# Rotary tables scaled per tile, a residual moved ahead of the maxima, and layer-norm statistics and root each moved one turn later

## The reference

```python
def ref(x, ...):
    xn = _layernorm(x)
    return x + attn(xn) + ffn(xn)        # attn: 16 heads of 8, causal, once

def ffn(x, ...):
    for i in range(6):                   # DEPTH
        x = attn_layer(shift_tokens(x), Wqkv[i], q_scale[i], k_scale[i], Wo[i]) + x
        x = ffn_layer(shift_tokens(x), ln_g[i], ln_b[i], W1[i], b1[i], W2[i], b2[i]) + x
    return x

def attn_layer(x, Wqkv, qs, ksc, Wo):    # 16 heads of 64, windows of 32
    q, k, v = split(x @ Wqkv)
    q, k = l2norm(q) * qs, l2norm(k) * ksc
    q = q * cos * scale + rotate_half(q) * sin * scale
    k = k * cos / scale + rotate_half(k) * sin / scale
    return local_attention(q, k, v) @ Wo # softmax over own and previous window

def ffn_layer(x, g, bln, W1, b1, W2, b2):
    xn = (x - mean(x)) / sqrt(var(x) + 1e-5) * g + bln
    a, gate = split(xn @ W1 + b1)
    return a * gelu(gate) @ W2 + b2
```

## Time and profile before

| what | value |
|---|---|
| median of 3 runs | 2076.58 us (2074.1 to 2080.54) |
| the profiled execution | 2091.56 us |
| its span | 2089.8 us |
| TensorE matmul busy | 91% of the span |
| VectorE busy | 80% |
| GpSimd busy | 70% |
| ScalarE busy | 63% |

### The profile page before, as it was taken

The page is one execution under the profiler, slowest core; times in us unless marked ns, Lnnn a source line. Parts: engine busy times, 40 slices in busy tenths (PEclk is TensorE's granted clock), DMA queues, the critical chain, the costliest instruction groups (busy, mean ns, idle before and its releaser), DMA issues.

```text
span 2089.8 us, 74558 instructions
## 1 busy us (share of the span) xinstructions
PE 1909.8 (91%) x32776; PEld 1295.6 (62%) x32776; DVE 1670.1 (80%) x1819; ACT 1310.5 (63%) x1723; POOL 1459.1 (70%) x1467
## 2 busy tenths in 40 slices
PE   3989997689999999999889999999998999999985
PEld 1334443357776667777656677767676776676774
DVE  5777661688888899888978988889888888988862
ACT  1366665466766676666656766776676667766752
POOL 1011113999888889888868888888887888888820
PEclk7699999799999999999999999999999999999998
DMA  3141100233333323333223323233332333222221
GB/s 105 41 140 41 60 11 21 51 79 71 74 85 75 89 67 82 89 75 87 64 51 86 94 72 92 70 88 84 76 85 66 81 89 76 70 65 66 68 68 46
DMA packets 144035, 151.51 MB, mean 73 GB/s; under 512 B 60760, under 2 KB 85596, under 8 KB 142944
## 3 DMA queue, kind: packets, MB, share of 16 engines
q1 hardware_dynamic: 143712, 146.75, 27.9%
HBM read 35.75 MB, written 5.44 MB: 20 GB/s over the span
## 4 chain that ended last, share of the span: by engine, by line
PE 32%; DVE 24%; POOL 20%; issue 15%; SPq 4%; ACT 4%; DMA 1%; POOLq 0%; DVEq 0%; ACTq 0%
POOL arena L1138 8%; POOL arena L1146 5%; PE banks L484 4%; DVE ss L731 4%; DVE arena L642 4%; PE banks L421 3%; SPq L1302 3%; PE banks L578 3%; PE banks L551 3%; PE banks L511 3%; DVE mx_t L766 3%; DVE arena L739 3%; DVE arena L780 2%; PE banks L493 2%; PE banks L561 2%
## 5 line engine op out<-in xcount | busy, mean ns | idle before, releaser
L1138 POOL TENSOR_TENSOR arena<-arena,tab_sl 128x512 f32<-128x512 f32 x384 | 590.0, 1567 | 17.2 <-ACT arena L938 10.8
L1146 POOL TENSOR_TENSOR arena<-arena 128x1024 f32<-128x1024 f32 x192 | 489.0, 2568 | 0.0
L739 DVE TENSOR_TENSOR arena<-arena,rn 128x1024 f32<-128x1024 f32 x192 | 360.6, 1919 | 110.9 <-POOL rn L1114 110.9
L484 PE MATMUL banks<-w_qkv,arena 128*128 128x512 f32 x768 | 362.0, 615 | 9.7 <-ACT arena L930 7.2
L967 ACT ACTIVATE arena<-arena 128x1024 f32<-128x1024 f32 x96 | 101.5, 1057 | 410.7 <-DVE arena L770 410.7
L551 PE MATMUL banks<-arena 64*64 64x32 f32 x12288 | 243.0, 222 | 2.0 <-DVE arena L770 1.8
L484 PEld LDWEIGHTS banks<-w_qkv,arena 128*128 128x128 f32 x768 | 141.1, 193 | 163.2 <-issue 154.3
L551 PEld LDWEIGHTS banks<-arena 64*64 64x64 f32 x12288 | 232.2, 134 | 14.6 <-DVE arena L770 2.8
L780 DVE TENSOR_TENSOR arena<-banks,tab_cl 128x1024 f32<-128x1024 f32 x192 | 226.3, 1219 | 14.0 <-ACT arena L938 12.2
L642 DVE TENSOR_REDUCE arena<-banks 128x1 f32<-128x512 f32 (+3 forms) x352 | 183.3, 586 | 66.5 <-PE banks L381 57.4
L1080 POOL TENSOR_SCALAR_AFFINE_SELECT arena<-arena 128x512 f32<-128x512 f32 x64 | 40.9, 640 | 267.7 <-ACT arena L888 267.5
(11 more groups left out here) (108 smaller groups left out, 2985.9 us busy)
## 6 DMA issues: line engine op xcount, KB each, us to landing
arena<-arena SPq DMA_DIRECT2D x1512, 64.0 KB
arena<-parts_dram SPq DMA_DIRECT2D x64, 144.0 KB
w_qkv<-Wqkv SPq DMA_DIRECT2D x6, 1024.0 KB
parts_dram<-arena SPq DMA_DIRECT2D x12, 256.0 KB, 3.0
tab_cl<-tab_c SPq DMA_DIRECT2D x6, 512.0 KB, 7.1
tab_sl<-tab_s SPq DMA_DIRECT2D x6, 512.0 KB
w_o<-Wo SPq DMA_DIRECT2D x6, 512.0 KB
w_qkv<-Wqkv SPq DMA_DIRECT2D x6, 512.0 KB, 4.4
```

What stands on the lines that cost most here:

```text
L484: last = e.matmul(ps[:, BANK * c:BANK * (c + 1)], xsT[b][:, P * t:P * (t + 1)], w_qkv[:, at:at + BANK], start=True, stop=True)
L739: e.tensor_tensor(to, to, rn[n // 2 % 2][:, n % 2, HEADS * m:HEADS * (m + 1)].unsqueeze(2).to_broadcast([P, HEADS, HEAD_DIM]), ALU.mult).t ...
L1138: e.tensor_tensor(qk_sw[:, m, :].rearrange("p (h d) -> p h d", d=HEAD_DIM)[:, :, d:d + HALF], raw[:, m, :].rearrange("p (h d) -> p h d", d ...
L1146: e.tensor_tensor(to, to, qk_sw[:, m, :], ALU.add).then_inc(S["rs"], 1)
```

## The change

Four edits, all in the second part.

- `scale_cos` and `scale_sin` become `scale_tables(l, t)`, which scales one tile t of both tables with three instructions: one over 2 x 64 values, two over 2 x 32. For the first layer all 8 tiles are scaled ahead of the second part. For the others tile t is scaled in step 7 + t of the layer before, so in steps 7 to 14, after `rotate` and `first_values` and ahead of `norms`. The counts of `tab_c` and `tab_s` that others wait for are multiplied by 8.
- On VectorE `ff_residual` stands ahead of `subtract` in turn 1, no longer behind it.
- `ff_stats` stands at the end of turn 2, no longer at the end of turn 1.
- On GpSimd `ff_rsqrt` stands at the head of turn 3, ahead of `rotate`; it stood in turn 2 between `rotate` and `norms`.

```diff
@@ vector_program
             def rotate(n):
                 l, b, t = of_tile(n)
-                w.wait_ge(S["tab_c"], l + 1)
+                w.wait_ge(S["tab_c"], tiles * (l + 1))
...
                     scale(s - 3)
+                if s >= FF and k == 1 and G > 0:
+                    ff_residual(G - 1)
                 if 0 <= s - 4 < n_tiles:
                     subtract(s - 4)
-                if s >= FF and k == 1 and G > 0:
-                    ff_residual(G - 1)
...
-                if ff_here and k == 1:
+                if ff_here and k == 2:
                     ff_stats(G)
@@ gpsimd_program
-            def scale_cos(l):
+            def scale_tables(l, t):
                 w.wait_ge(S["gain0_in"], 16 * (l + 1))
                 w.wait_ge(S["gain1_in"], 16 * (l + 1))
                 w.wait_ge(S["cos_in"], 16 * (l + 1))
-                tab = tab_cl[l % 2][:, :, :, :]
-                e.tensor_tensor(tab, tab, qk_gain[:, :, :].unsqueeze(1).to_broadcast([P, tiles, 2, HEAD_DIM]), ALU.mult).then_inc(S["tab_c"], 1)
-
-            def scale_sin(l):
-                w.wait_ge(S["gain0_in"], 16 * (l + 1))
-                w.wait_ge(S["gain1_in"], 16 * (l + 1))
                 w.wait_ge(S["sin_in"], 16 * (l + 1))
+                tab = tab_cl[l % 2][:, t, :, :]
+                e.tensor_tensor(tab, tab, qk_gain[:, :, :], ALU.mult).then_inc(S["tab_c"], 1)
                 for d, o in ((0, HALF), (HALF, 0)):
-                    tab = tab_sl[l % 2][:, :, :, d:d + HALF]
-                    e.tensor_tensor(tab, tab, qk_gain[:, :, o:o + HALF].unsqueeze(1).to_broadcast([P, tiles, 2, HALF]), ALU.mult
-                                    ).then_inc(S["tab_s"], 1)
+                    tab = tab_sl[l % 2][:, t, :, d:d + HALF]
+                    e.tensor_tensor(tab, tab, qk_gain[:, :, o:o + HALF], ALU.mult).then_inc(S["tab_s"], 1)
...
+                if s >= FF and k == 3 and G < n_groups:
+                    ff_rsqrt(G)
                 if 0 <= s - 1 < n_tiles:
                     rotate(s - 1)
-                if s % all_tiles == 7 and s // all_tiles + 1 < layers:
-                    scale_cos(s // all_tiles + 1)
-                if s % all_tiles == 9 and s // all_tiles + 1 < layers:
-                    scale_sin(s // all_tiles + 1)
                 if 0 <= s - 2 < n_tiles and (s - 2) % tiles == 0:
                     first_values(s - 2)
-                if s >= FF and k == 2 and G < n_groups:
-                    ff_rsqrt(G)
+                if 7 <= s % all_tiles < 7 + tiles and s // all_tiles + 1 < layers:
+                    scale_tables(s // all_tiles + 1, s % all_tiles - 7)
                 if 0 <= s - 1 < n_tiles and s % 2 == 0:
                     norms((s - 2) // 2)
```

More of the change, by code:

```diff
@@ L1082, in gpsimd_program @@
                 w.wait_ge(S["a_causal"], quad + 1)
-            scale_cos(0)
-            scale_sin(0)
+            for t in range(tiles):
+                scale_tables(0, t)
             w.wait_ge(S["ya_out"], 16 * batches)
-            w.wait_ge(S["tab_s"], 2)
+            w.wait_ge(S["tab_s"], 2 * tiles)
             for b in range(batches):
@@ L1132, in rotate @@
                 raw = qk_raw[n % 2]
-                w.wait_ge(S["tab_s"], 2 * (l + 1))
+                w.wait_ge(S["tab_s"], 2 * tiles * (l + 1))
                 w.wait_ge(S["rs"], 2 * n)
@@ L1199, in load_gains @@
             def load_gains(l):
-                w.wait_ge(S["tab_s"], 2 * l)
-                w.wait_ge(S["tab_c"], l)
+                w.wait_ge(S["tab_s"], 2 * tiles * l)
+                w.wait_ge(S["tab_c"], tiles * l)
                 for m, name in enumerate(("q_scale", "k_scale")):
```

## The result

The changed kernel takes 2108.62 us (median of 4 runs, 2090.99 to 2117.89), the kernel before beside it 2078.56 us (4 runs, 2074.10 to 2080.66). The ratio is 1.0136, with a 95% interval of 1.0095 to 1.0178: slower, by less than 2%, where 2053 us and faster was forecast. The profiled execution took 2117.89 us, the longest of the four, with a span of 2116.2 us.

The account below looks back on a forecast made before the run. TensorE, busy 91% of the span, was taken as the bound, with waits for VectorE in turns 1 and 2. Turn 2's -28.8 us and the tables' +5.2 made -23.6, from the median 2053 us; range 2044 to 2064.

Parts of the forecast that it names:

- What bounds turn 2, and the gain: TensorE waits in turn 2 for VectorE, held back 2.05 us by the statistics; moving them gains 18 x 1.6 = 28.8 us.
- late groups: Every second group of four steps: GpSimd's norms come late and VectorE's L739 of turn 1 waits 5.09 us for them.
- lockouts: VectorE's L759 kept out during GpSimd's whole string of rotations, 9 us and more; seen three times before, TensorE waiting 6.88 us.
- The tables, in work: GpSimd's table sets: step 10's delays the norms of a late group by 1.04 us in 5 layers, 5.2 us lost.
- The root: GpSimd's root moved to turn 3, taking 1.93 us, up to 3.6: cost nothing, or up to 1 us in a turn 3.
- The residual: VectorE's residual ahead of the maxima in turn 1: L561's 0.86 us wait returns as a wait of L532, worth 0.
- the sum -28.8 + 5.2: Turn 2's gain plus the tables' cost, -23.6 us in all, taken from the median to give 2053.0 us.
- the rival of many lockouts: Table sets and moved rotations lock VectorE out of L759 many more times: 2085 to 2190 us, chance 0.18.
- The rival's 2115 us: If 3 in 10 of all 40 table sets are hit, nine more lockouts of 6.88 us, 62 us.
- The rule of the Trainium skill: Whoever of VectorE and GpSimd issues first has SBUF for one instruction, so no 9 us stall of L759 could be: 2053.

Follow-up runs that it names:

- e9: The kernel before with one wait of GpSimd for its own instructions behind each of the two table scalings; 2072.30 us, ratio 0.9919.
- e5: The changed kernel with a wait of GpSimd for its own three instructions behind each table set; 2056.29 us, ratio 0.9888.
- e11: e5 with the statistics (`ff_stats`) at the end of turn 1 again, the root staying in turn 3; 2082.28 us.
- e8: e4 with the feed-forward residual behind the subtraction again; 2074.53 us.
- e4: The changed kernel with whole tables scaled ahead of the norms, cosines in step 6 and sines in step 14 of a layer; 2057.57 us, ratio 0.9859.
- e10: e1 with a wait of GpSimd for its own set behind each table set; 2089.40 us, ratio 0.9990.
- e3: The changed kernel without the scaling of the tables of layers 1 to 5, left out of the computation; 2057.78 us, ratio 0.9868.
- e12: e9 with the residual ahead of the maxima, as in the change; 2072.93 us.
- e1: The kernel before with the tables scaled tile by tile in steps 7 to 14 and nothing else changed; 2160.92 us, ratio 1.0372.
- e6: e4 with the wait ahead of a rotation split, so that GpSimd goes from sum to product without a pause in every step; 2077.22 us.
- e7: e3 with three memsets of about the same length into an unused place for each table set of layers 1 to 5; 2067.09 us.

## Why the prediction was wrong

- **What bounds turn 2, and the gain.** Right in late groups, lucky in the sum. 18 x 1.6 = 28.8 us was forecast; from e9 to e5, both free of lockouts, turn 2 gains 328.1 - 298.7 = 29.4. In the ten late groups it goes from 161.1 us to 144.3, 1.7 a step, and the statistics do it (e11; in e8, without the residual's move, it is 145.2). In the others the statistics and the root alone bring 167.0 to 164.3 (e8); only with the residual ahead is it 151.3 (e4). The prediction had put the residual at 0. The count of 18 was off too: of the 20 turns 2 from 594.76 to 1919.25, 15 last 15.9 to 16.1 us.
- **The tables, in work.** Between e9 and e5 turn 1 loses 5.3 us, nearly all in late groups (160.5 to 165.6 us); 5.2 was forecast, from the set of step 10, which stands just ahead of them. The size fits in this pair; with the tables alone (e9 to e10) it was 17 us by the medians, and turn 3, where the prediction had nothing for the sets, grew by 12 us as well as turn 1 by 14.
- **The root.** "Cost nothing; if the cover is gone, up to 1 us in a turn 3." The cover was gone: turn 3 went from 397.6 to 412.2, 14.6 us for 20 turns, within that 1 us a turn, but the sum had taken nothing for it. The sets don't make it (e3, without them, has 411.6); with the statistics back it is 405.4 (e11), and the residual alone leaves it at 398.5 (e12). So it is the price of the root and the statistics together, and no run moves the root alone. I had bounded the root at 3.6 us with L739 in between, and that is what it takes, from 1251.01 to 1254.60. But I held the start of ScalarE's normalisation against the exponents alone and didn't follow what comes behind: ScalarE's copy came late for L780, VectorE waited 0.55 us there, and L759 started behind a sum of GpSimd and took 2.36 us, not 1.5. GpSimd's root and VectorE behind it, after:

```profile
1251.01 1.06 POOL L1119 TENSOR_SCALAR ln_v<-mean_var 128x4 f32<-128x4 f32 x1 [1.30 <-issue]
...
1254.40 0.20 POOL L1124 TENSOR_TENSOR ln_m<-ln_m,ln_r 128x4 f32<-128x4 f32 x1
...
1258.26 2.35 DVE L780 TENSOR_TENSOR arena<-banks,tab_cl 128x1024 f32<-128x1024 f32 x2 [0.55 <-ACT arena L938]
...
1262.26 2.36 DVE L759 TENSOR_TENSOR arena<-arena,rs_o 128x1024 f32<-128x1024 f32 x1
```

- **The residual.** Wrong in its reasoning: "VectorE's own chain is not shorter" holds in late groups, where L561 no longer waited and L532 waited 0.93 us for L759, as was said. In the others the maxima had an idle 2.77 us in front of them, a row that I had quoted and not used for this step.
- **The lockouts.** This is the step that failed: the sum -28.8 + 5.2 has no term for more of them, as if their number stayed at that of before. The runs showed seven, where before had three, at 8.4 us each, and a wait that removes them takes the changed kernel from 2108.6 to 2056.3 us (e5). I saw the three long L759 (8.65 to 10.45 us, not all "9 us and more") and saw that all of them followed a scaling of the tables. But I gave the rival of many lockouts 0.18. Three hits in ten scalings and none in 38 other overlaps was evidence for a cause in the scaling, and the change put 20 sets in odd steps, where there had been ten scalings; more lockouts were the likeliest case.
- **The rival's 2115 us.** That 2108.6 lies near it is luck. It stood for nine more lockouts. Four more were seen, which the prediction's own numbers put at 2053 + 4 x 6.88 = 2080.5. Two errors make about half of the 28 us between. 6.88 us is TensorE's wait alone, and a lockout cost 8.4 (5.4 between e10 and e1, 65.2 us of span for twelve). And the gain without lockouts was less than 23.6 us. The rest stays open, since how many lockouts the median runs had isn't known.
- **The forecast's 2053 us.** That the changed kernel takes 2056.3 us without lockouts is in part luck too. The sum started from a median that had lockouts in it. From e9 to e5 the gain is 16.0 us by the medians, 10.2 by the spans and some 6 by the ratios, where 23.6 was forecast; the 14.6 us of turn 3 are the largest part of what was missing.
- **The rule of the Trainium skill.** In "SBUF — State Buffer", "Who interferes with whom", the one that comes second is blocked until the first one's instruction is over. A lockout over five to ten instructions isn't in it; e1 alone shows twelve. The measurement decides.

## What to carry to other kernels

Where VectorE and GpSimd both work on operands in SBUF, look at the longest instance of each VectorE instruction, not at its mean: an outlier that ends with the other engine's string is a lockout, and each one here began while GpSimd ran without a pause. A wait of GpSimd for its own last instruction cost 0.1 to 0.2 us a step here and took the changed kernel from 1.0136 of the kernel before to 0.9888 of it. Work added to an engine with idle time isn't free if it fills the gap from which another engine lives. And a forecast that comes out near the measured time isn't confirmed by it: check each term in a pair of kernels that differ in it alone.

## What the hardware showed that I had not expected

- VectorE's L759 stood for up to 10.8 us, over nine instructions of GpSimd (13.65 us in e6), while in e5 the same string let it in early (1.98 us for L759, with a pause of 0.13 us ahead of the string).
- TensorE's granted clock was 0.50 behind each of the seven waits for it, so that its next 3 to 5 us of work ran slow as well.
- A pause matters even though VectorE doesn't use it: L759 starts 0.23 us after the pause is over (1341.12 and 1341.35 in e5).
- Three memsets in place of three products brought lockouts too (three in e7), and the lockout was over while the memsets ran. None was in step 11, where products brought two in the changed kernel and five in e1.
- The spread of a kernel's times shrank with the wait, from 34 us in 31 runs of the kernel before to 10 us in 10. It isn't a sure sign: e12 spreads over 20 us, and its longest run, the profiled one, has no long L759.
- Open: why, without a pause, one string locks VectorE out and the next doesn't, with L759 at the same place in it (step 11 of the changed kernel: it starts 0.40 to 0.44 us into the first product in four layers and is long in two).
